# Mixer chain of a small vision tower: mixing matrices formed one step sooner and products issued two steps ahead, one masking operation per step, and three unread products of ones per step

## What is computed

```
gate, vraw, params = split(x @ w_in)            # 384, 384, 12 columns
v  = silu(causal_conv4(vraw))                   # T x 384, as 6 heads of 64: u
B, C = l2norm(v @ w_bc), split in 6 heads of 8  # T x 6 x 8 each
# per head, with scalars d, a, s of each token:
z  = s * (z - d*a*xs + d * B[:, None] * u[None, :])
xs = xs + d * z                                 # both 8 x 64, T steps in sequence
y  = C @ xs
out = ((y + D_skip * u) * silu(gate)) @ w_out
```

## Time and profile before

| | |
|---|---|
| median of 3 runs | 1847.76 us (1836.61 to 1849.02) |
| profiled execution: its own time | 1847.83 us |
| its span, first to last instruction | 1846.0 us |
| mean granted TensorE clock | 0.847 |
| busy: TensorE, VectorE, ScalarE, GpSimd | 82%, 71%, 57%, 22% of the span |
| `mixer_bc`, `mixer_chain`, `to_tokens` begin at | about 477, 527.3, 655.3 us |

### The profile page before, as it was taken

How to read it: one execution, slowest core, us unless ns; L and a number is a source line. 1 busy time by engine, 2 the same in 40 slices (tenths; PEclk the granted TensorE clock), 3 DMA queues, 4 the chain that set the end, 5 groups by cost and what they waited for, 6 DMA issues and landing times. The chain is left out here.

```text
span 1846.0 us, 36517 instructions
## 1 busy us (share of the span) xinstructions
PE 1513.2 (82%) x14190; PEld 1135.7 (62%) x14190; DVE 1306.5 (71%) x2831; ACT 1053.0 (57%) x1872; POOL 411.4 (22%) x428
## 2 busy tenths in 40 slices
PE   5898995877349987899999854998198899999795
PEld 5888985776326675764444544888086554446474
DVE  5988895489646655837999375887365469995666
ACT  6988994433356616444998423665100548896455
POOL 0000000000357711036980013665000320000100
PEclk9999997688555588987999756999598889999898
DMA  5120001000000010002540092121200000000101
GB/s 138 27 65 23 14 2 48 1 4 1 1 7 1 1 33 1 14 1 104 180 131 2 1 271 66 56 62 50 73 1 5 9 2 2 2 2 2 33 1 35
DMA packets 52725, 67.96 MB, mean 37 GB/s; under 512 B 11511, under 2 KB 41465, under 8 KB 52554
## 3 DMA queue, kind: packets, MB, share of 16 engines
q1 hardware_dynamic: 46586, 50.74, 9.0%
q0 software_dynamic: 3840, 9.18, 1.7%
q10 hardware_dynamic: 2128, 5.71, 1.2%
HBM read 46.97 MB, written 18.65 MB: 36 GB/s over the span
## 5 line engine op out<-in xcount | busy, mean ns | idle before, releaser
L2007 DVE TENSOR_REDUCE att_max<-banks 104x1 f32<-104x512 f32 (+1 forms) x480 | 295.9, 682 | 9.7 <-PE banks L1921 5.7
L2042 ACT ACTIVATE att_p<-banks 104x514 f32<-104x514 f32 (+1 forms) x480 | 262.3, 600 | 33.3 <-PE banks L1966 22.6
L339 PE MATMUL banks<-tok_wT,feature_halves 128*128 128x192 f16 x2592 | 229.5, 249 | 22.9 <-DVE feature_halves L365 11.8
L339 PEld LDWEIGHTS banks<-tok_wT,feature_halves 128*128 128x128 f16 x2592 | 217.4, 99 | 31.8 <-DVE feature_halves L365 17.5
L1982 PE MATMUL banks<-att_p,att_v 104*32 104x257 f32 (+1 forms) x1920 | 159.8, 405 | 0.9 <-ACT att_p L2042 0.3
L1966 PE MATMUL banks<-att_q,att_kT 64*104 64x257 f16 (+1 forms) x960 | 155.9, 304 | 2.9 <-ACT att_p L2042 2.5
L1921 PE MATMUL banks<-att_kT,att_q 64*104 64x512 f16 (+1 forms) x480 | 126.3, 424 | 4.9 <-DVE att_max L2007 2.1
L365 DVE TENSOR_TENSOR feature_halves<-features,feature_halves 128x2048 f16<-128x2048 f32 x54 | 123.4, 2285 | 6.1 <-ACT feature_halves L462 6.1
L1966 PEld LDWEIGHTS banks<-att_q,att_kT 64*104 64x104 f16 (+1 forms) x960 | 61.8, 123 | 107.0 <-ACT att_p L2042 80.2
L1146 POOL MEMSET C_start_apart<- 96x5472 f32 x1 | 4.7, 4658 | 476.0 <-POOLq L972 476.0
L462 ACT CAST feature_halves<-features 128x2048 f16<-128x2048 f32 x54 | 102.2, 1893 | 10.8 <-PE banks L339 10.0
(11 more groups left out here) (463 smaller groups left out, 3532.6 us busy)
## 6 DMA issues: line engine op xcount, KB each, us to landing
expert_w_in<-in_L_ffn_w_dram SPq DMA_DIRECT2D x16, 576.0 KB, 4.5
expert_w_halves<-expert_w_halves SPq DMA_DIRECT2D x32, 288.0 KB, 2.5
tok_w<-in_L_tok_W_dram ACTq DMA_DIRECT2D x4, 1152.0 KB, 7.3
expert_w2s<-expert_w_halves SPq DMA_DIRECT2D x1, 4608.0 KB
expert_y<-expert_out SPq DMA_DIRECT2D x6, 513.0 KB
expert_w1s<-expert_w_halves SPq DMA_DIRECT2D x2, 1536.0 KB
raw<-in_x_dram SPq DMA_DIRECT2D x2, 1152.0 KB, 5.7
expert_w1s<-expert_w_halves SPq DMA_DIRECT2D x3, 768.0 KB
```

What stands on the lines that cost most here:

```text
L339: ins = pe.matmul(c.bank[t // 2][:, (t % 2) * D:(t % 2 + 1) * D], fh[:, s, q, z, t * 128:(t + 1) * 128], wT[:, y, k, 6 * q + wf, :], start ...
L2007: dve.reduce_max(mx[0:qn, n // NS % 2, 2 * gi + e, k:k + 1], bank_of(unit)[0:qn, 0:KEYS], X).then_inc(maxed, 1)
L2042: act.activation(p[0:kn, n % 4, :, :], c.pair[2 + n % 2][0:kn, :].rearrange("p (e q) -> p e q", e=2)[:, :, 0:HALF], ACT.Exp, scale=scale). ...
```

## The change

In `mixer_bc`, B high is now written twice (`half.b`, rows 0 and 64 on) and B low once (`half.bl`, rows 64 on zero); C high stands once in `half.ch`, and C low in rows 64 on of the same tile. So one masked tile `cbd` holds both halves of C, and GpSimd masks once per step. The two products of a step are now `half.b` with `cbd` and `half.bl` with `cbd`. In the chain TensorE turns u and forms the products of C and B two steps ahead, ScalarE takes both high halves of step n + 1 before the `D_skip` multiplications of step n, and VectorE forms the matrix of step n + 2 at the end of iteration n. Ahead of every pair of products stand three products of ones, and 36 of them at the beginning of the chain. Since `half.bl` lies on the row of ones, GpSimd writes half of that row again as the last thing in the chain. GpSimd's order of `cbd(n)`, `transition(n)`, `gate(n - 2)` stays.

```diff
 # mixer_bc, gpsimd
+            pool.memset(half.bl[32:64, :], 0.0).then_inc(zeroed, 1)
             pool.memset(half.wh[32:64, :], 0.0).then_inc(zeroed, 1)
+            pool.memset(half.bl[64:112, :], 0.0).then_inc(zeroed, 1)
...
 # mixer_bc, scalar
                 if kind == 0:
                     act.copy(half.b[0:48, cols], ps[0:48]).then_inc(high, 1)
+                    act.copy(half.b[64:112, cols], ps[0:48]).then_inc(high, 1)
                 elif kind == 1:
                     act.copy(half.ch[0:48, cols], ps[0:48]).then_inc(high, 1)
-                    act.copy(half.ch[64:112, cols], ps[0:48]).then_inc(high, 1)
...
 # mixer_bc, vector
-                dve.wait_ge(high, n - 4 if kind == 0 else 5 + 2 * (n - 9))
+                dve.wait_ge(high, 2 * (n - 4) if kind == 0 else n + 1)
...
 # mixer_chain, gpsimd
                 pool.memset(wl[r:r + r, :, :, :], 0.0).then_inc(padded, 1)
-                pool.memset(cbl[r:(64, 112)[r // 64], :, :, :], 0.0).then_inc(padded, 1)
...
                 if n >= 2:
                     pool.wait_ge(cb_done, n - 1)
-                pool.tensor_tensor(cbh[:, n % 2, :, :], half.ch[:, cols]...
-                pool.tensor_tensor(cbl[0:48, n % 2, :, :], half.cl[:, cols]...
+                pool.tensor_tensor(cbd[:, n % 2, :, :], half.ch[:, cols]...
...
             for n in (N - 2, N - 1):
                 gate(n)
+            pool.wait_ge(cb_done, N)
+            pool.memset(c.xT[DH:DH + 1, 1, 0:NT // 2], 1.0).then_inc(ones_row, 1)
...
 # mixer_chain, scalar
+            act.wait_ge(init, 2)
+            highs(0)
+            for n in range(N):
+                if n + 1 < N:
+                    highs(n + 1)          # u_high, then wh twice
+                for k in range(3): ...    # D_skip of step n
...
 # mixer_chain, tensor
             def c_times_b(n):
-                pe.wait_ge(cbd_ready, 2 * n + 2)
+                pe.wait_ge(cbd_ready, n + 1)
                 if n >= 2:
                     pe.wait_ge(wt_ready, n - 1)
+                spin(c, pe, 3, 2 + n % 2)
-                pe.matmul(ps, half.b[:, cols], cbh...)
-                pe.matmul(ps, half.b[:, cols], cbl...)
+                pe.matmul(ps, half.b[:, cols], cbd...)
+                pe.matmul(ps, half.bl[:, cols], cbd...)
             turn(0)
+            turn(1)
+            spin(c, pe, 36, 4)
             c_times_b(0)
+            c_times_b(1)
             for n, (ch, b, bc_) in enumerate(steps):
-                if n + 1 < N:
-                    turn(n + 1)
+                if n + 2 < N:
+                    turn(n + 2)
...
-                if n + 1 < N:
-                    c_times_b(n + 1)
+                if n + 2 < N:
+                    c_times_b(n + 2)
...
 # mixer_chain, vector
-            prepare(0)
+            matrix(0)
+            u_low_part(0)
+            matrix(1)
             low_part(0)
             for n, (ch, b, bc_) in enumerate(steps):
                 if n + 1 < N:
-                    prepare(n + 1)
+                    u_low_part(n + 1)
...
                 # state(n), low_part(n + 1), y_plus_Du(n) as before
+                if n + 2 < N:
+                    matrix(n + 2)
```

More of the change, by code:

```diff
@@ L125, in bc, with spin @@
     return ap.broadcast_to(shape)
-def spin(c, pe, n):
+def spin(c, pe, n, bank=7):
     ones = c.ones[:, :].bitcast(F16)
     for _ in range(n):
-        pe.matmul(c.bank[7][:, 0:256], ones[:, 0:128], ones, start=True, stop=True)
+        pe.matmul(c.bank[bank][:, 0:256], ones[:, 0:128], ones, start=True, stop=True)
 def load_shared(c, out_ctx):
@@ L758, in mixer @@
         half.ch = place[0][0:112, NT:2 * NT]
-        half.cl = place[1][0:48, 0:NT]
+        half.bl = place[1][0:112, 0:NT]
         half.wh = c.sb(ctx, "B_end_high", [128, NBC * 96], F16)
@@ L1161, in _ @@
             act.activation(sr[0:L, :], ss[0:L, :], ACT.Sqrt).then_inc(rt, 1)
-            act.wait_ge(zeroed, 4)
+            act.wait_ge(zeroed, 5)
             for n in range(len(jobs)):
@@ L1204, in low_part @@
                 kind, cols, ps = job(n)
-                dve.wait_ge(high, n - 4 if kind == 0 else 5 + 2 * (n - 9))
+                dve.wait_ge(high, 2 * (n - 4) if kind == 0 else n + 1)
                 if kind == 0:
-                    dst, hi = half.b[64:112, cols], half.b[0:48, cols]
+                    dst, hi = half.bl[0:48, cols], half.b[0:48, cols]
                 else:
-                    dst, hi = half.cl[:, cols], half.ch[0:48, cols]
+                    dst, hi = half.ch[64:112, cols], half.ch[0:48, cols]
                 dve.tensor_tensor(dst, ps[0:48], hi, ALU.subtract).then_inc(low, 1)
@@ L1245, in mixer_chain @@
      s_done, s_ready) = map(c.sem, names)
-    skipped, padded = (c.sem(q) for q in ("Du_ready", "chain_padded"))
+    skipped, padded, ones_row = (c.sem(q) for q in ("Du_ready", "chain_padded", "ones_row_again"))
     N = NBC
@@ L1281, in _ @@
                     pool.wait_ge(cb_done, n - 1)
-                pool.tensor_tensor(cbh[:, n % 2, :, :], half.ch[:, cols].unsqueeze(1).broadcast_to((112, SH, L)),
+                if n:
+                    pool.wait_ge(cbd_ready, n)
+                pool.tensor_tensor(cbd[:, n % 2, :, :], half.ch[:, cols].unsqueeze(1).broadcast_to((112, SH, L)),
                                    mask[:, :].unsqueeze(2).broadcast_to((112, SH, L)), ALU.mult).then_inc(cbd_ready, 1)
[L1284 to L1290, removed]
+                pool.wait_ge(cbd_ready, n + 1)
                 if n < last:
@@ L1302, in _, with highs @@
                 gate(n)
+            pool.wait_ge(cb_done, N)
+            pool.memset(c.xT[DH:DH + 1, 1, 0:NT // 2], 1.0).then_inc(ones_row, 1)
         @block.scalar
         def _(act):
-            act.wait_ge(init, 2)
-            for n in range(N):
+            def highs(n):
                 act.wait_ge(u_t, n + 1)
@@ L1316, in _ @@
                     act.copy(wh[r:r + L, n % 2, :, :], wt[:, n % 2, :, :]).then_inc(wt_high, 1)
+            act.wait_ge(init, 2)
[3 more added lines that the diff above has]
+                    highs(n + 1)
+                cols = slice(steps[n][2] * L, (steps[n][2] + 1) * L)
+                if n + 2 < N:
+                    act.wait_ge(u_t, n + 1)
                 for k in range(3):
@@ L1335, in c_times_b @@
                 ps = c.bank[2 + n % 2][0:L, 0:SH * L]
-                pe.matmul(ps, half.b[:, cols], cbh[:, n % 2, :, :].rearrange("p a b -> p (a b)"),
+                spin(c, pe, 3, 2 + n % 2)
+                pe.matmul(ps, half.b[:, cols], cbd[:, n % 2, :, :].rearrange("p a b -> p (a b)"),
                           start=True, stop=False)
-                pe.matmul(ps, half.b[:, cols], cbl[:, n % 2, :, :].rearrange("p a b -> p (a b)"),
+                pe.matmul(ps, half.bl[:, cols], cbd[:, n % 2, :, :].rearrange("p a b -> p (a b)"),
                           start=False, stop=True).then_inc(cb_done, 1)
             turn(0)
-            pe.wait_ge(padded, 4)
+            turn(1)
+            spin(c, pe, 36, 4)
+            pe.wait_ge(padded, 2)
             c_times_b(0)
+            c_times_b(1)
             for n, (ch, b, bc_) in enumerate(steps):
@@ L1380, in _, with u_low_part @@
         def _(dve):
-            def prepare(n):
-                ch, b, bc_ = steps[n]
+            def u_low_part(n):
                 dve.wait_ge(u_high, n + 1)
@@ L1387, in prepare, with matrix @@
                                   ).then_inc(u_low, 1)
+            def matrix(n):
+                ch, b, bc_ = steps[n]
                 dve.wait_ge(cb_done, n + 1)
```

10 lines of the change are left out of this document (4 added, 6 removed).

## The result

The changed kernel takes 1878.4 us (median of 4 runs, 1874.3 to 1889.6) against 1845.0 (median of 4, 1836.6 to 1849.0) of the kernel before: ratio 1.0197, 95% interval 1.0138 to 1.0256: slower, by about 2%. Forecast: 1887 us. The profiled execution took 1876.7 us, its span is 1874.9.

A forecast was written before the change was run, and what follows sets the result against it. A ScalarE-VectorE ring of 3.32 us a step bounds the chain, replaced by a 4.55 us ring at half clock. Steps +35.9 less about 1, start +1.2, end +0.9, mixer_bc +2.1: +39.1 on 1847.8 gives 1887 us, range 1855 to 1896.

The forecast's parts named there:

- The new ring: Chain step: B times u, state, low part, y_plus_Du, gate, mask, ones, products in series; 4.55 us half clock, 3.78 full.
- The steps: Chain: 31 intervals of 4.55 us and about 11 for the last four, less about 1 for first steps at full clock.
- The clock: Chain: raised by the 36 ones, falls within the first chunks and stays down; the forecast case, chance 0.52.
- Start of the chain: Before y of step 0: the ones, first products and matrix work delay it from 9.4 to some 10.6 us, +1.2.
- `mixer_bc`: Stage ahead of the chain: five copies of B before the last low part, unhidden; +2.1 us, bounds 1.4 to 2.6.
- End: Chain's end: GpSimd's memset of the row of ones lies fully on the path before to_tokens; +0.9 us.
- The sum: Whole kernel: steps, start, end and mixer_bc together make +39.1 us, from 1847.8 to 1887 us.
- The signs: Changed profile: TensorE held by the mask, GpSimd by y_plus_Du, 4.5 us steps, clock falling to 0.50, mix_matrix wait gone.
- The bound before: Chain step of 3.32 us set by a ring of ScalarE and VectorE without TensorE; TensorE close second at 3.17.
- half clock without the ring: Rival for the chain: gate not ahead of mask in practice, TensorE binds at 3.81 us a step; 1869 us, chance 0.04.
- the clock holds: Rival: the chain keeps full clock, ring 3.78 us a step; 1860 us, range 1854 to 1868, chance 0.29.
- The other side: Rival: no ring and full clock, chain step about 3.0 us; 1838 us, faster, chance 0.05.

The follow-up runs named there:

- e1: Changed kernel with GpSimd masking C of step n + 1 ahead of transition and gate of iteration n; 1825.4 us, ratio 0.990 to the kernel before.
- e2: Changed kernel without the three products of ones in each step, the 36 at the beginning kept; 1862.8 us, ratio 1.010 to the kernel before.
- e4: Changed kernel with VectorE making y_plus_Du of step n before the low part of step n + 1; 1854.4 us, ratio 1.005 to the kernel before.
- e7: Changed kernel with GpSimd gating step n - 3 instead of n - 2 in iteration n; 1837.3 us, ratio 0.997 to the kernel before.
- e8: Changed kernel with six products of ones in each step instead of three; 1873.6 us, ratio 1.017 to the kernel before.
- e10: Changed kernel with the three ones of each step issued before TensorE's wait for the mask; 1842.7 us, ratio 1.000 to the kernel before.
- e5: Kernel before plus 36 products of ones ahead of the chain and three in each step; 1845.1 us, ratio 1.003 to the kernel before.
- e6: e1 plus GpSimd making B high's second copy in one piece and writing the ones row before the last two gates; 1817.7 us, ratio 0.988.
- e9: e6 plus VectorE forming the matrix of n + 2 ahead of the low part and y_plus_Du; 1808.9 us, ratio 0.981 to the kernel before.
- e3: Changed kernel with the mask one step sooner and no ones in the steps; 1842.0 us, ratio 0.997 to the kernel before.

## Why the prediction was right, point by point

- **The new ring** was right in every member and in its sum: 4.55 forecast, 4.54 measured at half clock; 3.78 forecast for full clock, 3.81 and 3.79 in the two steps at 631 to 638 us. The members were less exact than the sum: the low part 0.55 for 0.43, the ones 0.75 for 0.64, and against that 0.65 for 0.85 from B times u to the low part and 0.81 for 0.86 at the mask. The upper bound that I gave the low part, 0.62, is what its instruction takes above. e1, e2, e4, e7, e8 and e10 each change one member, and the step follows.
- **The steps**: forecast +34.9 us from the first y product of step 0 to that of step 35; measured 688.61 - 538.64 = 149.97 for 116.26, +33.7. Of the 31 steps forecast with the whole ring at half clock two were at full clock, with 3.8, and the first took 4.03 (by `y_plus_Du`).
- **The clock**: it rose with the 36 ones, fell in the first chunk and stayed down, save for two steps. The forecast case came in, in all four executions by their mean clock (0.841 to 0.851, and 0.849 in the profiled one), but the reason I gave was weak and part of that was luck. I had put TensorE at work for 1.7 to 2.1 of 3.78 us (45 to 56%); the profile shows it busy for 4.64 of 6.70 (69%). e5, e4, e7 and e10 keep 1.00 in stretches of 40 to 96 us with TensorE busy 68 to 75% of the time; after lost it twice at 73% and 69%. So the busy share does not decide between them. Those four also lost it once, at 542 to 546 us, and got it back 10 to 20 us later; of all runs only e1, e6 and e9, with the mask sooner and the ones, kept it until the last 4 us of the chain. What exactly decides stays open.
- **Start of the chain**: mis-sized. +1.2 forecast for the first y product, +0.45 measured. I had 6.1 us for the 36 ones alone; with the first three of the steps they took 5.43 (530.07 to 535.50), as the clock rose after 2.2 of them.
- **`mixer_bc`** +2.1 forecast, +2.35 measured. **End** +0.9 forecast; from the first y product of step 35 to `to_tokens` 3.31 us for 2.37, +0.94 (the memset is 0.95 long). **`to_tokens`** 0 forecast for this case, -0.63 measured.
- **The sum**: 39.1 forecast for the stages, 36.8 measured: the steps explain 1.2 of it, the start 0.75, `to_tokens` 0.6, `mixer_bc` and the end -0.3 together. The other 6 us between 1887 and the median are no part of the mechanism: 2.8 of them because I started from 1847.8 while the median of the four runs before is 1845.0, the rest in the unchanged part of the kernel and the scatter of runs.
- **The signs**: TensorE held ahead of its ones by GpSimd's mask, GpSimd ahead of the gate by `y_plus_Du`, and steps of 4.5 us are there. ScalarE's wait for `mix_matrix` is not gone, as I had said, but halved (0.55 us a step); ScalarE is busy 48% of the time there, and its wait is not in the new ring.
- **The bound before**: ring and TensorE were equal (e3: 3.31 by TensorE alone; e5: 3.32 by the ring alone). "TensorE is a close second, 3.17" was too low, without effect on the forecast, as neither binds after. The rival "half clock without the ring" would have had to be 3.31 + 0.64 = 3.95, or about 1874 us, nearer to the measured time than the forecast is: the total could not have told it from the ring, the step and e1 do.
- **Rivals**: "the clock holds" had the right price of a step (3.78 for 3.80 in the two steps at full clock and 3.78 + 0.33 for 4.13 in e8). The other side, faster, needed the mask out of the ring, and was then a larger gain (e1: -1.0%, step 2.68) than the step of 3.0 that I gave it.

## What to carry to other kernels

When products are moved a step ahead, everything that they wait for moves a step nearer to its own inputs: go through the in-order queue of the engine that makes the operand and see which older work it is behind, and on which step's results that waits. Here one mask that stayed behind a gate made a loss of 2% of a change that gains 1% once GpSimd's order is moved. Work that only keeps the clock up belongs ahead of the wait, where it fills the hold, not behind it, where it lengthens the ring; and it pays only once no other ring sets the step.

## What was unexpected in the hardware

The granted clock came back in mid-chain for 7 us, 631.3 to 638.0, without any change in the program, and went again; executions of one kernel differ in it (e4 and e8). With three products of 128x256 ones a step the clock is 1.00 from 552 us on in the order of before, with a wait of 1.09 us in the step shown (e5), while TensorE without a hole and without ones stays at 0.50 (e3). GpSimd's copy of 48x2052 f16 overlapped VectorE's 57x1728 f32 operation by 1.09 us and stretched it from 1.94 to 2.89 us, in e6 and in e9.
